# A three-layer GRU graph network on one Trainium2 core: the last four spans of the first layer summed edge by edge instead of through a weighted adjacency

## The reference

```python
for l in range(3):                       # layers 1 to 3, weighted
    m = x @ weight[l]
    agg = segment_sum(m[src] * edge_weight[:, None], dst)
    x = gru_cell(agg, x)
x = layernorm(x0 + x)
for W, b in ((W0, b0), (W1, b1), (W2, b2)):   # unweighted
    h = relu((h + segment_sum(h[src], dst)) @ W.T + b)
x = layernorm(x + h)
```

## Time and profile before

| | us |
|---|---|
| median of 3 runs | 2888.23 |
| the profiled execution, its own time | 2885.88 |
| its span, first to last instruction | 2884.1 |
| fused first layer, up to the first aggregation of layer 2 | 0 to 1023.5 |
| layers 2 and 3 | 1023.5 to about 2058 |
| the three unweighted layers | about 2058 to 2884 |

### The profile page before, as it was taken

How to read it: one execution, slowest core, us unless ns; L and a number is a source line. 1 busy time by engine, 2 the same in 40 slices (tenths; PEclk the granted TensorE clock), 3 DMA queues, 4 the chain that set the end, 5 groups by cost and what they waited for, 6 DMA issues and landing times.

```text
span 2884.1 us, 72504 instructions
## 1 busy us (share of the span) xinstructions
PE 2832.0 (98%) x29387; PEld 1880.8 (65%) x29387; DVE 1250.6 (43%) x2716; ACT 946.7 (33%) x1891; POOL 887.9 (31%) x1007
## 2 busy tenths in 40 slices
PE   6899999999999999999999999999999999999998
PEld 5899999999999965555555555555655555555554
DVE  7688888777888514344422344343500010001011
ACT  6677777777777610000001011101400010001111
POOL 4244444444444315454541454544100000000000
PEclk8999999999999999999999999999999999999999
DMA  5666666666662299998996988988488868886884
GB/s 197 244 261 262 245 244 262 261 257 241 252 262 114 96 405 347 341 335 338 356 366 255 343 335 329 360 332 324 150 325 301 310 248 302 308 304 247 318 304 161
DMA packets 134009, 810.64 MB, mean 281 GB/s; under 512 B 17208, under 2 KB 27308, under 8 KB 113948
## 3 DMA queue, kind: packets, MB, share of 16 engines
q1 hardware_dynamic: 111228, 758.32, 68.2%
q0 software_dynamic: 19968, 40.46, 4.3%
q10 hardware_dynamic: 2720, 10.62, 0.9%
HBM read 553.01 MB, written 256.33 MB: 281 GB/s over the span
## 4 chain that ended last, share of the span: by engine, by line
PE 97%; ACT 1%; DVE 1%; DMA 1%; issue 1%; POOL 0%; DVEq 0%; POOLq 0%; ACTq 0%
PE ps L969 31%; PE ps L1165 27%; PE ps L1247 19%; PE ps L1240 11%; PE ps L979 1%; PE ps L980 1%; PE ps L1260 1%; PE ps L1261 1%; PE ps L982 1%; PE ps L981 1%; PE ps L1144 1%; ACT ring L1661 1%; DMA x_keep<-xT 0%; PE ps L1267 0%; PE ps L1266 0%
## 5 line engine op out<-in xcount | busy, mean ns | idle before, releaser
L969 PE MATMUL ps<-ring,Y 128*128 128x448 f32 x2352 | 888.4, 539 | 0.0
L1165 PE MATMUL ps<-ring,Y 128*128 128x448 f16 x4116 | 780.6, 352 | 0.0
L1661 ACT ACTIVATE ring<-ps 128x490 f16<-128x490 f32 (+1 forms) x1344 | 698.1, 653 | 182.8 <-PE ps L1240 175.5
L969 PEld LDWEIGHTS ps<-ring,Y 128*128 128x128 f32 x2352 | 446.4, 190 | 434.8 <-issue 434.8
L1165 PEld LDWEIGHTS ps<-ring,Y 128*128 128x128 f16 x4116 | 402.8, 98 | 373.8
L863 POOL DMA_INDIRECT ring<-y_rows,ring x448 | 431.6, 963 | 518.0 <-PE ps L969 261.8
L1247 PE MATMUL ps<-ring,Y 128*128 (+1 forms) x2744 | 571.8, 360 | 0.4 <-ACT shared L1620 0.4
L1247 PEld LDWEIGHTS ps<-ring,Y 128*128 128x128 f32 x2744 | 504.8, 190 | 8.7 <-ACT shared L1620 0.8
L1240 PEld LDWEIGHTS ps<-shared 64*128 64x128 bf16 x18816 | 320.0, 93 | 83.5 <-issue 65.4
L1240 PE MATMUL ps<-shared 64*128 64x49 bf16 (+1 forms) x18816 | 345.6, 189 | 24.2 <-DVE shared L2142 15.5
L1824 DVE TENSOR_SCALAR ring<-ring 128x128 f32<-128x128 f32 x446 | 130.6, 293 | 389.5 <-DMA ring<-y_rows,ring 254.2
(11 more groups left out here) (196 smaller groups left out, 1449.6 us busy)
## 6 DMA issues: line engine op xcount, KB each, us to landing
ring<-adj_w SPq DMA_DIRECT2D x72, 2688.0 KB, 11.9
ring<-adj_h SPq DMA_DIRECT2D x42, 2800.0 KB, 9.4
ring<-adj_h SPq DMA_DIRECT2D x42, 2688.0 KB, 9.3
adj_w<-ring SPq DMA_DIRECT2D x48, 2016.0 KB, 11.8
adj_h<-ring SPq DMA_DIRECT2D x56, 1372.0 KB, 5.0
ring<-adj_w SPq DMA_DIRECT2D x24, 2912.0 KB, 10.3
adj_w<-ring SPq DMA_DIRECT2D x48, 728.0 KB, 6.8
sum_rows<-ring SPq DMA_DIRECT2D x62, 448.0 KB
```

Source lines behind the costliest of these rows:

```text
L969: mm = pe.matmul(ps[:, bank, 0:GW], Y[:, h, :], slab(s)[:, :, h - h0, :], start=(h == 0), stop=(last and h == TILES - 1))
L1165: mm = pe.matmul(ps[:, par, 0:GW], part[:, h, :], counts_slab(par, s)[:, :, h - h0, :], start=(h == 0 and part is Y_high), stop=(h == TILE ...
L1661: act.activation(strip[:, :, c0:c0 + UNIT * WIN].rearrange("p h (d j) -> p d h j", d=WIN)[:, :, :, w0:w1], psum_unit(a)[:, :, kind, :, :]. ...
```

## The change

- `ORDER` builds spans 24 to 27 first, in slots 0 to 3, **with counts only** (`build_counts`, `has_weights`): no weight parts (no L2142, two column steps instead of seven), 28 matmuls in a batch instead of 84, three evictions instead of six, no `adj_w` strips, no `add_tiles`. In these slots TensorE waits before each batch until all units of the batch before are evicted. The turning of x moves from batches 4 to 14 to batches 12 to 22.
- Slots 4 to 27 build spans 0 to 23. In slots 5 to 23 (`RUN_SLOTS`), batches 0 to 3, three **rounds** each of running sums over the rows of x run beside the building: GpSimd gathers (`fetch_batch`), ScalarE scales three batches later (`scale_rows`), VectorE adds in place five batches later (`sum_batch`), SyncE stores four rounds at a time. That is 12 rounds a slot, 224 in all.
- `place_ends` runs before VectorE's slot 25, `fetch_ends` in slots 25 and 26, `join_ends` in slot 26 and after slot 27. The gates lag further: slot t runs gate n = t - 6, and `GATE_ORDER` has spans 0 to 22, 24 to 27, 23. The tail has the gates of six spans between pieces of the 49 tiles (`TAIL_TILES`), and a `flip_run` for each of the four spans.
- ScalarE, VectorE, GpSimd and SyncE have their slots unrolled. TensorE keeps loops for slots 6 to 27; 41 `sem_inc` follow each count slot (`LOOP_LEAD` = 164).
- The edge list is loaded at the start into its own buffer; rounds use 16 buffers in place (`RUN_BUFS`), for all three layers. Stores are of four rounds; the last two of layers 2 and 3 are issued by GpSimd. W1, W2 and `gnn_weight` are loaded into the ring, and the descriptor scratch is set to 8192.
- VectorE waits for `x_keep` at the first blend (slot 6), no longer ahead of slot 2.

```diff
-ROW_BUFS = 10
-STORE = 7
+RUN_BUFS = 16
+STORE = 4
+FIRST_RUN = GATHERS - RUN_SPANS
+ORDER = [*range(FIRST_RUN, GATHERS), *range(FIRST_RUN)]
+GATE_ORDER = [*range(FIRST_RUN - 1), *range(FIRST_RUN, GATHERS), FIRST_RUN - 1]
+RUN_SLOTS = range(RUN_SPANS + 1, GATHERS - 4)
+RUN_BATCHES, RUN_PER_BATCH = 4, 3
+LAST_STORES = 2
+SCALE_LAG, SUM_LAG, STORE_LAG = 3, 5, 6
+PLACE_SLOT, ENDS_SLOT = 25, 25
+LOOP_LEAD = 164
+TAIL_TILES = [0, 6, 15, 24, 33, 42, TILES]
...
+            def fetch_round(turn, i):
+                if i >= RUN_BUFS:
+                    if i % STORE == 0:
+                        use, q = divmod(i // STORE - STORE_TURNS, STORE_TURNS)
+                        pool.wait_ge(s_stored[q], stored_by(turn, q) + 16 * (use + 1))
+                    pool.wait_ge(s_acc, RUN * turn + i - RUN_BUFS + 2)
+                pool.indirect_dma_start(out=run_bufs[:, i % RUN_BUFS, :], out_offset=None, in_=y_rows if turn else x,
...
+            def prepare_span(t):
+                par = t % 2
+                n = BATCHES * t
+                for k in range(2):
+                    fetch_batch(n + k)
...
+                add_own(t + 1, 1 - par)
+                take_places(t + 2, par)
+                if t in (ENDS_SLOT, ENDS_SLOT + 1):
+                    first = RUN_SPANS // 2 * (t - ENDS_SLOT)
+                    fetch_ends(0, range(first, first + RUN_SPANS // 2))
+                fetch_batch(n + 2)
+                for d, k in enumerate(FETCH_AT):
+                    pool.wait_ge(s_bmm, UNITS * (BUFS + n + k))
+                    gather(par, d)
+                    if d == 0:
+                        fetch_batch(n + k)
+                make_columns(t + 1, 1 - par)
+                near_rows(t + 3, 1 - par)
...
+            def build_counts(t):
+                pe.wait_ge(s_cola, t + 1)
+                for k in range(BATCHES):
...
+                    turn_inputs(n)
+                    pe.wait_ge(s_hot, hot_before(t, k + 1))
+                    pe.wait_ge(s_bev, evicted(t, k))
+                    for a in range(UNITS):
+                        build_unit(k % BUFS, a, False)
...
+            for t in range(RUN_SPANS):
+                build_counts(t)
+                for _ in range(LOOP_LEAD // RUN_SPANS):
+                    pe.sem_inc(s_mark_pe, 1)
             pe.wait_ge(s_xt, NC)
+            build_span(0, None, None, None)
+            build_span(1, 1, 0, None)
+            with pe.Fori(0, FIRST_RUN // 2 - 1) as i:
                 with pe.Fori(0, 2) as slot:
-                    build_span(2 * i + slot + 2, slot, 2 * i + slot)
+                    w = 2 * i + slot + 2
+                    build_span(w, slot, 2 * i + slot + 1, 2 * i + slot)
...
+            for c, n in enumerate(range(FIRST_RUN - 2, GATHERS)):
+                add_tiles(0, TAIL_TILES[c], TAIL_TILES[c + 1])
+                if n < GATHERS - 1:
+                    fused_gates(n)
...
+                if c < RUN_SPANS:
+                    flip_run(c)
...
+            def scale_rows(n):
+                for i in rounds_at(n):
+                    row = run_bufs[:, i % RUN_BUFS, :]
+                    act.wait_ge(s_row[i % RUN_BUFS], 16 * (i // RUN_BUFS + 1))
+                    act.activation(row, row, ACT.Copy, scale=run_edges[:, i, 1:2]).then_inc(s_prod if i else s_acc, 1)
...
+            def sum_row(turn, i):
+                done = RUN * turn + i
+                row, last = (run_bufs[:, j % RUN_BUFS, :] for j in (i, i - 1))
+                dve.wait_ge(s_acc, done)
+                dve.wait_ge(s_prod, done - turn)
+                dve.scalar_tensor_tensor(out=row, in0=last, scalar=run_edges[:, i, 2:3], in1=row,
+                                         op0=ALU.mult, op1=ALU.add).then_inc(s_acc, 1)
```

More of the change, by code:

```diff
@@ L370, in gnn_program @@
         N_IN = 15
-        N_CONST = 16
+        N_CONST = 19
         AHEAD = 2
@@ L437, in gnn_program, with end_buf @@
         hot = hot.bitcast(BF16).rearrange("p (b k w x) -> p b k w x", b=BUFS, w=BATCH, k=KINDS)
[L439 to L445, removed]
[L446 to L448 removed]
+        run_low = late[:, 0:RUN]
+        run_nodes = run_bufs[:, 0:2, :].rearrange("p b f -> p (b f)")[:, 0:RUN]
+        marks_at = LEAPS // 2 + 2
+        lane_firsts = shared[0:LANES, starts_at[-1]:starts_at[-1] + P // 2].bitcast(I16)[:, 0:P - 1]
+        lane_marks = late[0:LANES, marks_at:marks_at + P // 2].bitcast(BF16)[:, 0:P - 1]
+        def end_buf(span, d, part):
+            return 2 * (WIN * span + d) + part
+        assert end_buf(RUN_SPANS, 0, 0) <= RUN_BUFS and starts_at[-1] + P // 2 <= NODES + 6 * GW
         def sums_kept(b):
@@ new lines, in fetch_ends @@
+            def fetch_ends(turn, spans):
+                for b in range(STORES - LAST_STORES if turn else STORES, STORES):
+                    pool.wait_ge(s_acc, RUN * turn + STORE * (b + 1))
+                    pool.dma_start(sums_kept(b), sums_made(b)).then_inc(s_last, 16)
+                for q in range(STORE_TURNS):
+                    pool.wait_ge(s_stored[q], stored_by(turn + 1, q))
+                if turn:
+                    pool.wait_ge(s_last, 16 * LAST_STORES * turn)
+                if not turn:
+                    pool.wait_ge(s_place, PLACE_STEPS)
+                    pool.wait_ge(s_none, 32)
+                for span in spans:
+                    for d in range(WIN):
+                        for part in range(2):
+                            pool.indirect_dma_start(out=run_bufs[0:LANES, end_buf(span, d, part), :], out_offset=None,
+                                                    in_=sum_rows, in_offset=bass.IndirectOffsetOnAxis(
+                                                        ap=run_ends[:, part, d, span:span + 1], axis=0))\
+                                .then_inc(s_ends[span], 16)
@@ L849, in _ @@
+            for t in range(GATHERS):
+                prepare_span(t)
             pool.wait_ge(s_steps, WIN * (GATHERS + 2))
@@ L896, in _ @@
                     fetch_rows(layer)
-                    fetch_ends(layer)
+                    fetch_ends(1 + layer, range(RUN_SPANS))
             with pool.Else():
@@ L1234, in build_unit @@
                             sums = psum_unit(a)[:, d, :, w - w0, :]
-                            if part == 0:
+                            if not weighted:
+                                rhs = hot[slots, buf, 0, w, 0:TILES]
+                                sums = sums[:, 0, :]
+                            elif part == 0:
                                 rhs = hot[slots, buf, 0:2, w, 0:TILES]
```

503 lines of the change are left out of this document (266 added, 237 removed).

## The result

The changed kernel takes 3066.39 us (median of 4 runs, 3047.21 to 3067.74), the kernel before 2888.39 us beside it: a ratio of 1.0602, 95% interval 1.0582 to 1.0622. It is 178 us slower. The forecast was 2847, the range ended at 2888.

A forecast was written before the change was run, and what follows sets the result against it. TensorE, busy 98% of the span, was taken as the bound. Start 24.8, count slots to 108.4, slots 5 to 23 to 804.9, slot 27 to 942.7 and tail 39.4 gave 982.1 against 1023.5: 2888.2 - 41.4 = 2847 us, range 2812 to 2888.

The forecast's parts named there:

- 41.4: Forecast gain in us: layer 2's first aggregation starts at 982.1 instead of 1023.5.
- laid out: Stage summed anew from 0 to layer 2's first aggregation, forecast at 982.1 us; the profiled 2885.88 us was its base.
- The sign that I had named: In slots 5 to 22, TensorE's idle time put down to VectorE, and VectorE's before L2137 to GpSimd's columns.
- the fourth: Rival: program sent to the fallback, or a moved loop body stalls on instruction fetch; 2880 to 2900 us, 4%.
- Start: TensorE's first small matmul, at 27.06 us before, comes at 24.8 with five column steps and one L2142 fewer.
- Count slots: Slots 0 to 3: 2.3 us a batch through TensorE-ScalarE hand-overs, 83.6 us in all, end at 108.4.
- The clock: TensorE's granted clock stays low until slot 5, about 0.5 to 0.7 in slots 0 to 3; costs 2 us.
- Tail: From slot 27's end to layer 2's first aggregation: 27.1 us before, 39.4 with four more spans of gates and flips.
- Slots 5 to 22: Full slots of 12 rounds take 35.2 us each, bound by GpSimd's fetches; eighteen make 633.6 us.
- the old work: GpSimd's work per slot besides fetches: 14.6 us busy and 4.2 of gaps, 18.8, less 2.2 of lost waits.
- the second rival: GpSimd fits and the sums are free: slots of 34.2 us, 2829, or 2819 with cheap count slots; 22%.
- the row of L780: GpSimd indirect DMA taking 1.58 us inside VectorE's L2139, against L762's 1.03 while VectorE is idle.

The follow-up runs named there:

- the same number spread: Changed kernel with its 164 increments spread over TensorE's waits in the count slots instead of standing behind them, loop still at its 5133rd instruction: 3051.87 us.
- place 5171: Changed kernel with 202 increments instead of 164, so TensorE's loop starts at the 5171st instruction of its program: 2850.85 us; 2835.36 us with the increments spread.
- the kernel with 202 spread: Changed kernel with 202 increments instead of 164, spread over TensorE's waits instead of standing behind the count slots: 2835.36 us, ratio 0.9822.
- 105 and 189 past a multiple of 256 instructions: Loop starts of the changed kernel: 105 with no increments (2925.55 us) and with 256 (2985.9 us), 189 with 84 increments (3073.88 us).
- 13, 31 or 51: Loop starts past a multiple of 256 in the changed kernel: 164 increments (3066.39 us), 182 spread (3045.62 us), 202 (2850.85 us).
- two runs at place 5133: Changed kernel with 164 increments, rows fetched by plain DMAs instead of GpSimd's indirect ones: by SyncE 2837.75 us, by GpSimd's own queue 2842.72 us.
- 3123: TensorE's loop start in the kernel before; with 12 useless indirect DMAs a slot and GpSimd's loop written out there: 3137.1 us.

## Why the prediction was wrong

**The step that failed** is one sentence: "The unrolled queues and the 164 `sem_inc` (in TensorE's waits for evictions) I cost at nothing." For the queues it gives no reason, for the increments a wrong one. The 164 increments cost in two ways. They stand behind a slot's last batch and not in a wait, gaps of some 6 us: slot 5's transposes stand at 132.64 us with them, at 121.54 without and at 123.68 with the same number spread. (The medians of 3066.39 and 3051.87 us differ by 15, which runs from 3034 to 3069 don't resolve.) And they set the place of the loop: 202 instead of 164 are worth 215 us with nothing else changed. The stalls cost the rest: GpSimd's indirect DMAs back to back held up TensorE's instructions, 10 us and more in each of 18 slots, 6 in the next and 21 in the two of `fetch_ends`. That it takes the written-out queue is shown in the kernel before (234 us); in the changed kernel, where that queue costs nothing at place 5171, it was not tried in a loop.

The profiled execution adds up: 2885.88 - 41.4 + 218.0 (first aggregation later than laid out) + 3.3 (later layers) = 3065.8. Of the 218, 10 lie ahead of slot 4, which starts at 118.33 instead of 108.4; slots 5 to 23 take 857.7 us instead of 668.0, which is 190; slots 25 and 26 have the 21; the rest, 3 us less than laid out, is in slot 4, slot 24 and the tail. The sign that I had named, TensorE's idle time put down to VectorE, didn't come: 139.8 us of it stand at issue.

**The rival that named it** was the fourth: a loop body that stalls on instruction fetch, 22 passes of a few us, 4%. It had the number of passes (21 were hit) and that the loop's start matters, but its total of 2880 to 2900 us leaves 1.5 to 2.4 us a pass, where mostly 10 to 14 were lost; and the stalls of the changed kernel move next to nothing on q8, so that they are fetches of instructions is not shown. The argument against it ("TensorE's loops show no such stall now") was drawn from a trace without the load: beside that loop GpSimd ran a loop too and issued one indirect DMA at a time.

**Start**: forecast 24.8 us, first small matmul at 24.41. **Count slots**: forecast 2.3 us a batch, measured 2.2; their end forecast at 108.4, 106.69 where the increments are out of the way. The clock was as forecast: 0.50 granted from 20 to 40 us, the level of 1.2 GHz, with TensorE busy 6.18 of 20 us. **Tail**: forecast 39.4, measured 38.0 (931.67 to 969.63 in the kernel with 202 spread), the edges of 1 us not needed.

**Slots 5 to 22**: forecast 35.2 us with GpSimd as the bound, 34.2 once the stalls are gone. GpSimd's side of it, in the kernel with 202 spread (window of slot 13; group by line, 200 to 900 us):

```profile
506.70:540.90 34.20, 34.20 (x787) 31.74 (x786) 31.64 (x56) 29.85 (x67) 27.26 (x28) 1.00 0.76 297
L887 POOL DMA_INDIRECT run_bufs<-in_x,run_edges x200 | 257.4, 1287 | 77.7 <-issue 47.4 <-POOL take_now L831 11.9 <-DMA sum_rows<-run_bufs 6.3
```

A fetch takes 1.29 us and 0.30 of gap, 1.59; I had 1.55. What I had too high is the old work: 34.2 - 12 x 1.59 leaves 15.1 us at most for it, and I took 16.6. So the second rival (34.2, 22%) was nearer than the forecast, by 18 us, and half of these are eaten by the loop's first passes: 796.2 us from slot 5's transposes to the last, 9.6 more than 23 x 34.2. VectorE's and ScalarE's busy times were 31.6 and 29.9, forecast 32.3 and 30. On that kernel, whose increments lie in waits and whose place is free of stalls, the first aggregation comes at 969.63 instead of 982.1 us and what follows takes 1862.1 instead of 1860.6: 2846.8 - 12.5 + 1.4 = 2835.7, measured 2835.36. So the rest of the layout was 12 us too long in all.

**The page on SBUF.** By the inference in the Trainium skill (page "SBUF — State Buffer", section "Who interferes with whom"), that descriptor generation is not held up by `tensor_tensor`, each fetch would have taken 1.25 us with its gap. The fetches bear out the row of L780 instead: 1.29 us in the mean without the gap, between 0.94 and 1.89. In slot 13 of the kernel with 202 spread the longest ones (1.72 to 1.87) start inside VectorE's tensor-tensor operations; that these hold them up is read from the times, no run here takes them away.

## What to carry to other kernels

Before an engine's loop is written out, or instructions are put ahead of a loop, count where the long loop of the busiest engine comes to lie, and give the place itself a run: here 38 idle instructions were worth 215 us, more than the change. A queue that is written out is not free for the others: GpSimd in a loop bore 12 indirect DMAs a slot without a trace on TensorE, the same queue written out cost 10 us a slot there, and in the changed kernel nothing or as much, by the place of TensorE's loop. And an absence of stalls in the trace of before says nothing of a load that this trace doesn't hold; the cheapest test is to put the load, without its use, into the old kernel.

## What the runs showed of the hardware

- TensorE's loop of 1662 instructions stays on the chip: from 200 to 900 us the kernel before moved no packet on q8. The Trainium skill (page "Runtime: NRT & Kernel Launch", section "Instruction fetch mechanics") says that a taken branch to a target outside a window of two pages forces a fetch; that is not what this trace shows, since the branch goes back over six such blocks some 20 times in that stretch. By the same section's figures for TensorE, 128 KiB in blocks of 16 KiB, the memory would hold eight blocks, and the place with eight touched blocks is the one that loaded about 9 a slot. That the block that is fetched ahead drives one out at 105 past, where seven are touched, is a guess.
- Stalls on instructions come in two kinds. One has up to 5.9 us at a time and packets of 16 KB on q8, and came at 105 and 189 past a multiple of 256 instructions, not, beyond the loop's first passes, at 13, 31 or 51. The other has mostly 0.4 to 0.5 us at a time, 0.75 us apart with up to 6 matmuls between, and next to no packets (0 to 6 from 200 to 900 us); in every run that had it GpSimd's queue was written out and issued indirect DMAs back to back, and plain DMAs by the same queue did not bring it (2842.72 us).
- That the indirect DMAs and the small matmuls fall together is not enough. In slot 13 of the kernel with 202 spread the batch of 527.96 us runs in one piece beside a fetch of 528.20; the eight DMAs of `fetch_ends` spare TensorE in two runs at place 5133; and in layers 2 and 3 of the changed kernel GpSimd issues eight of them 0.3 us apart (from 1400.48 us) while TensorE, with long matmuls, waits on issue nowhere from 1200 to 2200 us.
- How a written-out GpSimd and indirect DMAs reach TensorE, and why 5171 is spared and 3123 is not, stays open. No run here tells it; GpSimd's queue in a loop within the changed kernel, the obvious next one, wasn't tried.
